# The output projection of a grouped-query attention layer in three rounded products, its weights split on chip

## What is computed

```python
q = (hidden_states @ Wq).reshape(b, s, NH, HD)      # NH = 32, HD = 128
k = (hidden_states @ Wk).reshape(b, s, NKV, HD)     # NKV = 4
v = (hidden_states @ Wv).reshape(b, s, NKV, HD)
q = _rms_norm(q, q_norm_w)
k = _rms_norm(k, k_norm_w)
...
q, k = _apply_rope(q, k, cos, sin)
k = jnp.repeat(k, groups, axis=1)
v = jnp.repeat(v, groups, axis=1)
scores = jnp.einsum('bhqd,bhkd->bhqk', q, k) * scaling
scores = jnp.where(causal[None, None], scores, jnp.finfo(scores.dtype).min)
attn = jax.nn.softmax(scores.astype(jnp.float32), axis=-1).astype(q.dtype)
out = jnp.einsum('bhqk,bhkd->bhqd', attn, v)
out = jnp.transpose(out, (0, 2, 1, 3)).reshape(b, s, NH * HD)
return out @ Wo
```

## Time and profile before

| | before |
|---|---|
| median of three runs | 1963.71 us |
| the profiled execution | 1964.2 us |
| its span, first to last instruction | 1962.4 us |
| mean granted TensorE clock over the span | 0.892 |
| TensorE busy over the span | 1561.5 us (80%) |
| VectorE busy | 1258.8 us (64%) |
| ScalarE busy | 922.2 us (47%) |
| GpSimd busy | 660.6 us (34%) |

### The profile page before, as it was taken

One profiled execution on the slowest core, in us unless ns is written; L12 is line 12 of the kernel. 1 busy time (PEld: TensorE's weight loads), 2 busy tenths in 40 slices (PEclk: granted clock), 3 DMA queues, 4 the chain that ended last, 5 costly groups with the idle time before them and its releaser, 6 DMA issues. The chain is left out here.

```text
span 1962.4 us, 28135 instructions
## 1 busy us (share of the span) xinstructions
PE 1561.5 (80%) x9150; PEld 1212.3 (62%) x9158; DVE 1258.8 (64%) x2128; ACT 922.2 (47%) x2281; POOL 660.6 (34%) x671
## 2 busy tenths in 40 slices
PE   6899789779864655191679999999999999998372
PEld 4444578667751223191668888888888888886262
DVE  3665454656466998355657777777777777776533
ACT  2365335234424332251556665666666666664341
POOL 3011260315066764605822222222222222220703
PEclk9899799889977888595889999999999999999586
DMA  3221333223410001444000000000000000000543
GB/s 77 50 50 63 95 112 115 73 70 97 125 54 0 0 1 51 143 132 135 11 0 12 12 12 8 16 1 23 1 23 1 23 1 12 1 1 1 161 145 97
DMA packets 75323, 98.29 MB, mean 50 GB/s; under 512 B 11168, under 2 KB 58912, under 8 KB 75184
## 3 DMA queue, kind: packets, MB, share of 16 engines
q1 hardware_dynamic: 69040, 79.71, 13.8%
q0 software_dynamic: 6144, 16.79, 2.7%
HBM read 62.38 MB, written 27.66 MB: 46 GB/s over the span
## 5 line engine op out<-in xcount | busy, mean ns | idle before, releaser
L1112 ACT ACTIVATE gqa_probsT_high<-aux 128x512 fp32r<-128x512 f32 x288 | 172.7, 599 | 258.5 <-PE aux L1343 257.4
L1226 DVE TENSOR_REDUCE gqa_neg_max<-acc 128x1 f32<-128x1024 f32 (+7 forms) x256 | 192.5, 752 | 130.1 <-PE acc L1335 128.2
L1231 DVE TENSOR_TENSOR gqa_probsT_low<-aux,gqa_probsT_high 128x512 fp32r<-128x512 f32 x288 | 197.3, 685 | 90.9 <-ACT gqa_probsT_high L1112 89.7
L1121 ACT ACTIVATE gqa_probs<-acc,gqa_neg_max 128x1024 f32<-128x1024 f32 (+7 forms) x256 | 190.0, 742 | 39.0 <-DVE gqa_neg_max L1226 35.8
L1343 PE MATMUL aux<-ident,gqa_probs 128*128 128x128 f32 x1152 | 174.3, 274 | 0.0
L1019 POOL TENSOR_SCALAR gqa_q_scale<-gqa_q_scale 128x4 f32<-128x4 f32 x64 | 16.4, 256 | 437.6 <-ACT gqa_square L1056 437.3
L1354 PE MATMUL aux<-gqa_probsT_high,gqa_v_high 128*128 128x512 f32 x288 | 145.7, 506 | 1.6 <-ACT gqa_oT L1106 1.2
L1366 PE MATMUL aux<-gqa_wo,gqa_oT 128*128 128x256 f32 x512 | 134.3, 385 | 9.7 <-DVE stream L1219 8.9
L1333 PE MATMUL acc<-gqa_k_high,gqa_q_high 128*128 128x512 f32 (+5 forms) x384 | 130.7, 340 | 6.8 <-ACT gqa_probs L1121 5.2
L1333 PE MATMUL acc<-gqa_k_high,gqa_q_low 128*128 128x512 f32 (+5 forms) x384 | 132.0, 344 | 0.0
L1333 PE MATMUL acc<-gqa_k_low,gqa_q_high 128*128 128x512 f32 (+5 forms) x384 | 131.7, 343 | 0.0
(11 more groups left out here) (397 smaller groups left out, 4449.4 us busy)
## 6 DMA issues: line engine op xcount, KB each, us to landing
f_w<-in_f_up SPq DMA_DIRECT2D x64, 256.0 KB, 2.7
f_xs<-tokens_by_slot SPq DMA_DIRECT2D x108, 128.0 KB, 2.2
outputs_by_slot<-f_y_tile SPq DMA_DIRECT2D x108, 128.0 KB, 1.7
f_w<-in_f_down SPq DMA_DIRECT2D x64, 128.0 KB, 3.1
mat_qk<-mat_high SPq DMA_DIRECT2D x64, 64.0 KB, 2.3
gqa_w_q<-in_g_wq SPq DMA_DIRECT2D x8, 512.0 KB, 3.5
gqa_wo<-in_g_wo SPq DMA_DIRECT2D x8, 512.0 KB, 3.8
tokens_by_slot<-zeros SPq DMA_DIRECT2D x1, 3968.0 KB, 13.2
```

The source lines that it names most:

```text
L1112: act.activation(probsT_high[:, u % RING, :], aux[:, u % 2, :], ACT.Copy).then_inc(cell_high_ready, 1)
L1121: act.activation(out, scores(n), ACT.Exp, bias=neg_max[:, j % (2 * JOBS):j % (2 * JOBS) + 1], accum_out=row_sum[:, n // 2 % 4, m, n % 2:n ...
L1226: dve.tensor_reduce(neg_max[:, j % (2 * JOBS):j % (2 * JOBS) + 1], scores(n), AXY, ALU.max, negate=True).then_inc(max_ready, 1)
L1231: dve.tensor_tensor(probsT_low[:, u % RING, :], aux[:, u % 2, :], probsT_high[:, u % RING, :].bitcast(F32), ALU.subtract).then_inc(cell_lo ...
```

## The change

The output projection goes over to rounded parts. ScalarE's copy of the finished bank becomes `oT_high`, a rounded high part, and VectorE gets a new instruction at the head of the slot, `oT_low`, the bank less that high part. TensorE waits for `oT_low` where it waited for the copy, and takes each head's product in three rounded matmuls. The weights `wo` are split on chip in the same way by halves of a quad (two heads, 512 columns): high part on ScalarE and low part on VectorE, at the ends of slots 2 and 5 of the 896 band. The loaded weights and both parts have one buffer each; the load of the next quad waits for the low parts of this one. To make room, the ring of turned cells goes from four to three, and the early key and value weights move one of their four parts into `oT_high` and `oT_low`. Two hunks that only name semaphores are left out:

```diff
 
         sem = ctx.enter_context(Sems(nc, "gqa"))
         norm = Norm(nc, core, ctx, sem, "gqa", whole=False)
-        RING = 4
+        RING = 3
         w_q = sb("w_q", [P, DC * QUAD * HD])
         w_q_high = sb("w_q_high", [P, DC * QUAD * HD], F32R)
         w_q_low = sb("w_q_low", [P, DC * QUAD * HD], F32R)
-        wo = sb("wo", [P, 2, QUAD, D])
+        wo = sb("wo", [P, QUAD, D])
+        wo_high = sb("wo_high", [P, QUAD, D], F32R)
+        wo_low = sb("wo_low", [P, QUAD, D], F32R)
         norm_w = sb("norm_w", [P, 2, HD])
         below = sb("below", [P, P], BF16)
         ident_b = sb("ident_b", [P, P], BF16)
...
         neg_max = sb("neg_max", [P, 2 * JOBS])
         row_sum = sb("row_sum", [P, 4, QUAD, 2])
         row_inv = sb("row_inv", [P, 4, QUAD, 2])
-        oT = sb("oT", [P, 2, QUAD * P])
+        oT_high = sb("oT_high", [P, 2, QUAD * P], F32R)
+        oT_low = sb("oT_low", [P, 2, QUAD * P], F32R)
 
         early = probs[:, :, :].rearrange("p a b -> p (a b)")
         w_kv = early[:, 0:2048].rearrange("p (g n) -> p g n", g=KV)
...
         k_swapped = early[:, 6144:7168].rearrange("p (t d) -> p t d", d=HD)
         cos_k = early[:, 7168:8192].rearrange("p (t d) -> p t d", d=HD)
         sin_k = early[:, 8192:9216].rearrange("p (t d) -> p t d", d=HD)
-        w_kv_high, w_kv_low = probsT_high, probsT_low
+        w_kv_high = [probsT_high[:, 0, :], probsT_high[:, 1, :], probsT_high[:, 2, :], oT_high[:, 0, :]]
+        w_kv_low = [probsT_low[:, 0, :], probsT_low[:, 1, :], probsT_low[:, 2, :], oT_low[:, 0, :]]
         straight = norm.xn[:, 0:4, :].rearrange("p (r a) d -> p r (a d)", r=2)
         swapped = norm.xn[:, 4:8, :].rearrange("p (r a) d -> p r (a d)", r=2)
-        k_square = oT[:, :, :].rearrange("p a (t d) -> p (a t) d", d=HD)
+        k_square = wo_low[:, :, :].rearrange("p a (t d) -> p (a t) d", d=HD)
         cos_q = core.xnT[:, 0, :].rearrange("p (t d) -> p t d", d=HD)
         sin_q = core.xnT[:, 1, :].rearrange("p (t d) -> p t d", d=HD)
         A, B = slice(0, HD // 2), slice(HD // 2, HD)
...
             band, c = divmod(z, CELLS)
             return band // 4 + 1 if c == at and band % 4 == 2 and band // 4 + 1 < QUADS else None
 
+        def wo_part(z):
+
+            band, c = divmod(z, CELLS)
+            return (band // 4, {2: 0, 5: 1}[c]) if c in (2, 5) and band % 4 == 1 and band // 4 < QUADS else None
+
         block = ctx.enter_context(nc.Block())
 
         @block.sync
...
                 sp.dma_start(w_q[:, :], wq_dram[quad:quad + 1].rearrange("a p k n -> (a p) (k n)")).then_inc(w_q_in, 16)
 
             def load_wo(quad):
-                sp.dma_start(wo[:, quad % 2, :, :], wo_dram[quad:quad + 1].rearrange("a h p n -> p (a h) n")).then_inc(wo_in[quad % 2], 16)
+                sp.dma_start(wo[:, :, :], wo_dram[quad:quad + 1].rearrange("a h p n -> p (a h) n")).then_inc(wo_in, 16)
 
             sp.dma_start(w_kv, wkv_dram.rearrange("g p k n -> p g (k n)")).then_inc(w_kv_in, 16)
             load_q(0)
...
             sp.dma_start(core.xnT[:, 0, :], cos_dram.rearrange("p t d -> p (t d)")).then_inc(tables_in, 16)
             sp.dma_start(core.xnT[:, 1, :], sin_dram.rearrange("p t d -> p (t d)")).then_inc(tables_in, 16)
             load_wo(0)
-            load_wo(1)
             for quad in range(1, QUADS):
                 sp.wait_ge(w_q_low_ready, quad)
                 load_q(quad)
-                if quad >= 2:
-                    sp.wait_ge(wo_done, 2 * NT * (quad - 1))
-                    load_wo(quad)
+                sp.wait_ge(wo_low_ready, 2 * quad)
+                load_wo(quad)
 
         @block.gpsimd
         def _(pool):
...
 
             act.wait_ge(w_kv_in, 16)
             for g in range(KV):
-                act.activation(w_kv_high[:, g, :], w_kv[:, g, :], ACT.Copy).then_inc(w_kv_high_ready, 1)
+                act.activation(w_kv_high[g], w_kv[:, g, :], ACT.Copy).then_inc(w_kv_high_ready, 1)
             split_q(0)
             squares(0)
             read_kv(0)
...
                     act.wait_ge(weighed, last_cell(n) + 1)
                     if n >= 2:
                         act.wait_ge(wo_done, 2 * (n - 1))
-                    act.activation(oT[:, n % 2, :], out_bank, ACT.Copy).then_inc(oT_copied, 1)
+                    act.activation(oT_high[:, n % 2, :], out_bank, ACT.Copy).then_inc(oT_high_ready, 1)
                 u = z - CELLS
                 if 0 <= u < CELLS * BANDS:
                     act.wait_ge(cell_turned, u + 1)
...
                 quad = new_quad(z, 1)
                 if quad is not None:
                     split_q(quad)
+                if wo_part(z):
+                    quad, half = wo_part(z)
+                    act.wait_ge(wo_in, 16 * quad + 16)
+                    if quad >= 1:
+                        act.wait_ge(wo_done, 2 * NT * quad - 1 + half)
+                    act.activation(wo_high[:, 2 * half:2 * half + 2, :], wo[:, 2 * half:2 * half + 2, :], ACT.Copy).then_inc(wo_high_ready, 1)
 
         @block.vector
         def _(dve):
...
 
             for g in range(KV):
                 dve.wait_ge(w_kv_high_ready, g + 1)
-                dve.tensor_tensor(w_kv_low[:, g, :], w_kv[:, g, :], w_kv_high[:, g, :].bitcast(F32), ALU.subtract).then_inc(w_kv_low_ready, 1)
+                dve.tensor_tensor(w_kv_low[g], w_kv[:, g, :], w_kv_high[g].bitcast(F32), ALU.subtract).then_inc(w_kv_low_ready, 1)
             split_q(0)
             dve.wait_ge(q_tables_ready, 3)
             rope(0)
...
                                          core.x[:, t, :], ALU.mult, ALU.add).then_inc(added, 1)
 
             for z in range(SLOTS + 1):
+                for n in ended(z):
+                    dve.wait_ge(oT_high_ready, n + 1)
+                    dve.tensor_tensor(oT_low[:, n % 2, :], out_bank, oT_high[:, n % 2, :].bitcast(F32), ALU.subtract).then_inc(oT_low_ready, 1)
                 if z < SLOTS and job(z):
                     j, n, m = job(z)
                     dve.wait_ge(scored, j + 1)
...
                 quad = new_quad(z, 2)
                 if quad is not None:
                     split_q(quad)
+                if wo_part(z):
+                    quad, half = wo_part(z)
+                    dve.wait_ge(wo_high_ready, 2 * quad + half + 1)
+                    dve.tensor_tensor(wo_low[:, 2 * half:2 * half + 2, :], wo[:, 2 * half:2 * half + 2, :],
+                                      wo_high[:, 2 * half:2 * half + 2, :].bitcast(F32), ALU.subtract).then_inc(wo_low_ready, 1)
 
         @block.tensor
         def _(pe):
...
                         tokens = slice(t * P, (t + 1) * P)
                         cols = slice(k * 2 * HD, (k + 1) * 2 * HD)
                         for m, (a, b) in enumerate(three(core.xnT_high[:, k, tokens], core.xnT_low[:, k, tokens],
-                                                         w_kv_high[:, g, cols], w_kv_low[:, g, cols])):
+                                                         w_kv_high[g][:, cols], w_kv_low[g][:, cols])):
                             last = pe.matmul(kv_banks[t // 2][:, t % 2 * 2 * HD:(t % 2 + 1) * 2 * HD], a, b,
                                              start=k + m == 0, stop=(k, m) == (DC - 1, 2))
                     if t % 2:
...
                 g = group_of(n)
                 pe.wait_ge(cell_low_ready, u + 1)
                 if s == 0 and n >= 1:
-                    pe.wait_ge(oT_copied, n)
+                    pe.wait_ge(oT_low_ready, n)
                 for c, (a, b) in enumerate(three(v_high[:, g, s, :], v_low[:, g, s, :],
                                                  probsT_high[:, u % RING, :], probsT_low[:, u % RING, :])):
                     last = pe.matmul(out_bank, a, b, start=s + c == 0, stop=(s, c) == (tile_of(n), 2))
...
 
             def project_out(n, half):
                 quad = n // NT
-                pe.wait_ge(oT_copied, n + 1)
-                if half == 0:
-                    pe.wait_ge(wo_in[quad % 2], 16 * (quad // 2) + 16)
+                pe.wait_ge(oT_low_ready, n + 1)
+                pe.wait_ge(wo_low_ready, 2 * quad + half + 1)
                 if 2 * n + half >= 1:
                     pe.wait_ge(added, 2 * (2 * n + half))
                 for m in range(2):
                     head = 2 * half + m
-                    last = pe.matmul(wo_bank[:, m * D:(m + 1) * D], oT[:, n % 2, head * P:(head + 1) * P], wo[:, quad % 2, head, :],
-                                     start=True, stop=True)
+                    rows = slice(head * P, (head + 1) * P)
+                    for c, (a, b) in enumerate(three(oT_high[:, n % 2, rows], oT_low[:, n % 2, rows], wo_high[:, head, :], wo_low[:, head, :])):
+                        last = pe.matmul(wo_bank[:, m * D:(m + 1) * D], a, b, start=c == 0, stop=c == 2)
                 last.then_inc(wo_done, 1)
 
             for z in range(SLOTS):
```

7 lines of the change are left out of this document (5 added, 2 removed).

## The result

| | before | after |
|---|---|---|
| median, us | 1964.12 (1961.83 to 1965.69) | 1983.91 (1981.19 to 1988.36) |
| ratio of the medians | 1 | 1.0104 [1.008, 1.0128] |
| the profiled execution, us | 1964.2 | 1981.84 |
| its span, us | 1962.4 | 1979.1 |
| mean granted TensorE clock | 0.892 | 0.892 |

The account below looks back on a forecast made before the run. TensorE's own stream, 97% busy, was taken as the bound; band terms -2.5+6.9+11.1+0.2+4.2 and +1 at the end made +21 us on 1964.2, so 1985.2, median 1984.7; range 1971 to 1997.

Parts of the forecast that it names:

- Slot 1: Odd tiles' end in each band: copy plus subtraction outlasts TensorE's cover, losing 0.12, 0.28, 0.44 and 0.61 us.
- The waits behind the query split: 768 band, slot 3, seven of eight quads: subtraction stands behind the 1.81 us query-weight split, TensorE 2.23 us later.
- the bare subtractions: Layer's end: three subtractions without scores to cover them, some 0.8 us each, against six groups at 0.17: +1 us.
- The 768 band: Net per band: 2.23 late in slot 3, less 0.30 and 0.34, gives +1.59 us seven times; last quad +0.2.
- The group's gain: TensorE's projection: six rounded matmuls at 0.70 us replace 0.87, saving 0.17 a group, 22 us over 128 groups.
- Slot 8's gain: Slot 8's group gains nothing, since the query projection behind it already waits for VectorE, 23 times; 4 us.
- No change: Rival: waits only in the 896 and 768 bands, 20 us, slot 1 covered, against 18 us gain: 1966; chance 5%.
- Slower by more: Rival: waits spread, each of 64 tiles costing TensorE the full 0.69+0.15 us: +32, 1996; chance 12%.
- the faster rival: Subtraction always done in time, TensorE's stream remains the bound, all but slot 8's share counts: -18 us, 1946; chance 8%.
- new waits: Sum over the kernel: the 22 us of TensorE work go, and some 43 us of new waits come.
- VectorE's added work: VectorE about 59 us busier: 64 subtractions at 0.69 and 16 weight-split subtractions at 0.91 us.
- The 1.81: VectorE's 1024-column query-weight split takes 1.81 us in the trace, where the skill's formula would give 1.22.

Follow-up runs that it names:

- the run in which nobody waits: Changed kernel, but VectorE's subtraction works on other data, same size and place, and TensorE waits only for ScalarE's copy: 1969.35 us.
- the kernel with the later projection: Changed kernel with the output projection's groups moved one place on and the weight splits moved to slots 5 and 7: 1996.86 us.
- the last version of the change: Changed kernel, query split and projection later, weight splits in slots 5 and 8, two ScalarE copies earlier, 896-band rotary products behind slot 2's subtraction: 1960.66 us.

## Why the prediction was right, point by point

**Sign, size and place were right.** 21 us were forecast, 19.8 measured, and they lie in the bands and slots named. Slot 1 loses 0.11, 0.28, 0.45 and 0.63 us in the 1024, 896, 768 and 640 bands (each the step in the table's yardstick between the masks of slots 1 and 2, with the group's own 0.15 added back) against 0.12, 0.28, 0.44 and 0.61. The waits behind the query split are there, seven times, passed in length only by one of 1.8 at the layer's start; the one in slot 2 of the 896 band is there in every quad (0.99 for the 1.2 that it was to cost together with slot 1's loss: 1.10 on that footing). At the layer's end the bare subtractions cost 0.9, forecast 1. That the total came within 1.2 us is in part luck: the gain of a group was taken too large and the 768 band too dear, and these two errors pull in opposite directions.

**The 768 band was 0.3 too dear**, the largest single miss (7 times, 2.2 us). On the prediction's footing the weighing in slot 3 comes 2.09 late, forecast 2.23; and slots 4, 5 and 6 give 0.81 back, where 0.30 for the query turn and 0.34 for the two groups were forecast. The way it goes was right; what is given back beside the turn and the groups wasn't resolved further.

**The group's gain was mis-sized:** 0.17 forecast, 0.14 to 0.15 measured in the bands of the kernel without the subtraction, where nothing new can wait. Over 128 groups that is 18.8 us, not 22. Most of the error is rounding, for the prediction's own rows give the smaller figure: 1.10 less 0.24 is 0.86, where it wrote 0.87, and six steps of 0.12 are 0.72, where it wrote 0.70; that leaves 0.14.

**Slot 8's gain is lost in all 32 bands, not in 23.** In every band of after the lead from slot 8 is back at zero by slot 1's mask, 4.7 us; 4 were written off.

**No change** took it that slot 1 is covered. It isn't: the chain of 0.62 and 0.69 behind the copy's start outlasts the score and the turn with VectorE idle. **Slower by more** needed each of the 64 tiles to cost the whole chain of 0.69 and 0.15; in the 1024 band slot 1 lost 0.11 and slot 5 nothing.

**The price of the faster rival was wrong, though not the chance.** 1946 took it that all of the gain but slot 8's reaches the end if nothing waits for the subtraction. Without the subtraction the kernel takes 1955.89. Of the 18.8, slot 8's groups lose 4.7, much as written off; the step of that sum which failed is that I read the existing waits as a fixed sum. In the 896 and 768 bands ScalarE's copy, the low part of the queries behind the weight split and the cell's low part behind the query split stood just at TensorE's pace, and took some 4.5 us more as soon as TensorE came earlier. Here 18.8 us off the engine that is 97% busy brought 9.5, and new work on the one at 74% turned that into a loss of 20. The Trainium skill (Perfetto Trace Analysis, Identifying the Most-Contended Engine) says to optimize the engine of the highest occupancy first, and to judge TensorE by its weight loads, not by its matmul time; by those too (632.85 of 780.00 us, 81%) it names TensorE, and here following it alone brought half of what was taken off TensorE.

**The waits were summed as if they stood side by side.** 40 us of waits on the subtraction were forecast; in after matmuls waited 29.4 us for it over the layer (us, times):

```profile
  PE aux L1378: 22.1, 23
  PEld aux L1391: 13.6, 25
  PE aux L1391: 7.3, 18
```

(the weight loads' 13.6 lie beside the matmuls' waits and aren't added). And the run in which nobody waits shows that they aren't the only thing that costs: take them away, and half of the loss stays, as waits for the cell's low part and in the query turn. The net per band came out right, since the prediction followed VectorE's list from start to start; the 43 us of "new waits" in its sum were a name for two things.

**VectorE's added work was 56 us by its rows, not 59**: 43.9 for 64 subtractions, 12.0 for the 16 weight splits (its busy time rose by 46.0 only: time that two neighbouring rows share counts once there, and its other rows are 3 us shorter). The splits took 0.75 us each on the mean; 0.91, half of the 1.81 for 1024 columns, was too high. These 12 us are hidden, as forecast: without them after doesn't change.

**The 1.81 was taken for the length of a split, and it isn't.** All seven query splits of that length begin while a GpSimd product of 1.04 us runs (L1027 before, L1037 after); in slot 3 none runs, and all seven take 1.21. The weight splits show the same: eight run alone and take 0.69 us, eight begin beside that product and take 0.79 to 0.94. The prediction says that the Trainium skill's formula (VectorE: DVE Perf Modes, The TRN2 errata), which gives 0.69 us for 512 columns and 1.22 for 1024, does not hold here; it holds for the splits that run alone.

**The granted clock** was to stay at 1.00 in the steady stretch, and did. In one of the experiments it fell (below), which the prediction allowed for only as a price it might have missed.

## What to carry to other kernels

When a matmul group is made cheaper by an operand that another engine has to prepare, price the group by the gap that is left after the waits already there, and then follow the preparing engine's list from the instruction that stands ahead of the new one: here a split of 1.81 us, in no hurry at all, was worth some 10 us by standing one slot early, two thirds of it through the new wait. Test a new instruction in two steps, once left out and once done without anybody waiting for it, since the work on the list and the wait for its result cost time separately and hide one another in a table of waits. And run the cheapest repair on the old kernel too, before its gain is put down to the new one.

## What was not expected of the hardware

VectorE's splits whose two operands both lie in SBUF ran longer whenever they began while GpSimd was multiplying: for 1024 columns 1.81 us in slot 2, beside the product, and 1.21 in slot 3, without it, seven of seven each; 0.79 to 0.94 instead of 0.69 for 512 in after, 1.41 and more where the subtraction is left out. The splits that read one operand from PSUM didn't: of the 288 cells' low parts in after, 90 ran beside a GpSimd instruction, and none took longer than 0.69. No run takes the GpSimd product away and leaves the rest, so the cause is argued from these rows, not shown by itself.

TensorE's granted clock fell towards half (to 1.2 GHz for most of the next 3.6 us) behind a wait of 2.05 to 2.07 us in the kernel with the later projection, in six quads of seven, and stayed at 1.00 behind the waits of 1.57 in after, in seven of seven. Both stand at the same place, behind the same kind of work and ahead of the same kind, though the kernel with the later projection has also waited 1.1 us at the band's start, where after waits 0.5. The length of the last wait doesn't decide it alone: the clock stayed at 1.00 behind 2.04 in the seventh quad, and in the last version of the change it fell behind a wait of 1.84 at the layer's start (0.57 from 1010.10 to 1014.10). What does decide it these runs don't show. Where it fell, a wait 0.5 us longer cost another 1.6, and a forecast that adds waits up in a straight line ends there.
